# Local attention: row sums of the second bank of probabilities as one VectorE reduce in place of ScalarE's accumulator

## The reference

```python
for i in range(6):
    x = attn_layer(shift_tokens(x), Wqkv[i], q_scale[i], k_scale[i], Wo[i]) + x
    x = ffn_layer(shift_tokens(x), ...) + x

def attn_layer(x, Wqkv, qs, ksc, Wo):          # 16 heads of 64
    q, k, v = split(x @ Wqkv)
    q = rotary(l2norm(q) * qs); k = rotary(l2norm(k) * ksc)
    sim = einsum('bhwie,bhwje->bhwij', bq, bk2) * 8.0       # windows of 32, and the one before
    sim = where(mask, -max, sim)
    attn = softmax(sim, -1)
    return einsum('bhwij,bhwje->bhwie', attn, bv2) @ Wo
```

## Time and profile before

| | |
|---|---|
| median of 3 runs | 3133.28 us (3121.46 to 3135.31) |
| the profiled execution | 3126.73 us, span 3124.9 us |
| PE busy | 2713.3 us, 87% of the span |
| DVE busy | 2025.1 us, 65% |
| ACT busy | 1984.1 us, 63% |
| POOL busy | 1581.3 us, 51% |
| DMA queues | 5.5% of the 16 engines' span for the largest |

### The profile page before, as it was taken

The page is one execution under the profiler, slowest core; times in us unless marked ns, Lnnn a source line. Parts: engine busy times, 40 slices in busy tenths (PEclk is TensorE's granted clock), DMA queues, the critical chain, the costliest instruction groups (busy, mean ns, idle before and its releaser), DMA issues. The chain is left out here.

```text
span 3124.9 us, 70010 instructions
## 1 busy us (share of the span) xinstructions
PE 2713.3 (87%) x27218; PEld 1731.6 (55%) x27218; DVE 2025.1 (65%) x3872; ACT 1984.1 (63%) x5960; POOL 1581.3 (51%) x1845
## 2 busy tenths in 40 slices
PE   5996998899988998899889988999879977996995
PEld 2554776467746775577647764777434434552552
DVE  3765887588847885788668865888345434645663
ACT  3445888488857886688758884888523333554343
POOL 0424877288827883688548872888133102310530
PEclk8898999999999999999999999999979987998797
DMA  2001000100010001000100001000000000000000
GB/s 97 2 2 45 17 17 17 42 17 17 17 40 19 17 17 37 21 19 17 40 17 17 18 15 42 17 18 17 31 7 1 2 0 0 2 1 0 1 2 14
DMA packets 35939, 57.93 MB, mean 19 GB/s; under 512 B 7200, under 2 KB 32800, under 8 KB 33952
## 3 DMA queue, kind: packets, MB, share of 16 engines
q1 hardware_dynamic: 35616, 53.52, 5.5%
HBM read 27.28 MB, written 1.05 MB: 9 GB/s over the span
## 5 line engine op out<-in xcount | busy, mean ns | idle before, releaser
L1051 POOL TENSOR_TENSOR l_qk<-l_ta,l_tb 128x256 f32<-128x256 f32 x768 | 539.9, 735 | 110.3 <-DVE l_tb L1105 110.3
L1067 POOL TENSOR_TENSOR l_qk<-l_qk,l_rn 128x512 f32<-128x512 f32 x384 | 392.7, 1044 | 217.3 <-DVE l_rn L1127 217.3
L674 POOL TENSOR_SCALAR qmr<-q_all,cf 128x256 fp32r<-128x256 f32 x128 | 116.1, 926 | 710.8 <-SPq L475 375.7
L706 DVE TENSOR_REDUCE mrow<-ring 128x2 f32<-128x512 f32 x512 | 324.3, 683 | 196.6 <-PE ring L522 184.1
L972 ACT ACTIVATE l_pr<-st,l_mn 128x128 f32<-128x128 f32 x1152 | 407.5, 382 | 35.7 <-DVE l_mn L1093 35.7
L1058 POOL TENSOR_TENSOR l_pr<-l_pr,l_rs 128x512 f32<-128x512 f32 x384 | 391.7, 1042 | 43.0 <-DVE l_rs L1117 43.0
L659 ACT ACTIVATE pt<-st 128x512 f32<-128x512 f32 x384 | 200.2, 600 | 288.4 <-PE st L557 288.4
L1109 DVE TENSOR_REDUCE l_n<-l_sq 128x8 f32<-128x512 f32 x384 | 262.8, 686 | 178.0 <-ACT l_sq L981 175.9
L972 ACT ACTIVATION_READ_ACCUMULATOR l_pr<-st,l_mn 128x1 f32 x1152 | 255.3, 222 | 0.0
L547 PE MATMUL st<-qm,k_all 32*128 32x512 f32 x1024 | 223.0, 673 | 0.0
L835 PE MATMUL ring<-l_wa,l_xs 128*128 128x512 f32 x384 | 194.0, 628 | 24.2 <-DMA l_wa<-in_wa 13.1
(11 more groups left out here) (237 smaller groups left out, 6380.3 us busy)
## 6 DMA issues: line engine op xcount, KB each, us to landing
l_vm<-l_v SPq DMA_DIRECT2D x192, 96.0 KB, 2.0
l_wa<-in_wa SPq DMA_DIRECT2D x7, 2048.0 KB, 9.5
l_vm<-l_v SPq DMA_DIRECT2D x192, 32.0 KB, 1.9
l_wf<-in_wf SPq DMA_DIRECT2D x6, 580.5 KB, 3.7
w<-in_w SPq DMA_DIRECT2D x1, 2752.0 KB, 16.1
cf<-in_cf SPq DMA_DIRECT2D x1, 1123.0 KB, 17.8
x<-in_xT SPq DMA_DIRECT2D x1, 1024.0 KB, 4.8
ctxT<-in_ctxT SPq DMA_DIRECT2D x1, 1024.0 KB, 8.6
```

Source lines behind the costliest of these rows:

```text
L706: dve.tensor_reduce(mrow[b % 2][:, t, j, 2 * p:2 * p + 2], bank_of(f"R{r}").rearrange("p (h k) -> p h k", h=2), AX.X, ALU.max).then_inc(ri ...
L1051: ins = pool.tensor_tensor(halves[0][:, :, x], halves[1][:, :, x], halves[2][:, :, 1 - x], ALU.add)
L1067: pool.tensor_tensor(part, part, t.rn[:, :, 4 * x:4 * x + 4].unsqueeze(3).broadcast_to([P, 2, 4, LHD]), ALU.mult).then_inc(qk_normed, 1)
```

## The change

ACT's exponentials of the first bank (hh = 0) keep their accumulator output. Those of the second bank (hh = 1) have none. DVE's `reciprocals` first reduces the 4 x 128 exponentials of the second bank in SBUF to 4 sums in one instruction, raises a new semaphore, waits for it, and then takes the reciprocals of all 8 sums as before.

```diff
-    recip_ready, p_normed = g.sem("l_reciprocals_ready"), g.sem("l_probs_normed")
+    sums_ready, recip_ready, p_normed = g.sem("l_row_sums_ready"), g.sem("l_reciprocals_ready"), g.sem("l_probs_normed")
@@ exps (ACT)
                 for x in range(4):
                     c, tile = divmod(x, 2)
+                    kw = {"accum_out": t.ps[:, u, hh, x:x + 1]} if hh == 0 else {}
                     ins = act.activation(t.pr[:, u, hh, c, tile, :],
                                          bank(g, f"R{hh}", k)[:, x * P:(x + 1) * P], ACT.Exp, scale=-1.0,
-                                         bias=t.mn[:, u, hh, x:x + 1], accum_out=t.ps[:, u, hh, x:x + 1])
+                                         bias=t.mn[:, u, hh, x:x + 1], **kw)
                 ins.then_inc(exps_done, 1)
@@ reciprocals (DVE)
             def reciprocals(N, k):
                 dve.wait_ge(exps_done, 2 * N + 2)
+                dve.tensor_reduce(t.ps[:, k % 2, 1, :], t.pr[:, k % 2, 1, :, :, :].rearrange("p c t q -> p (c t) q"),
+                                  AX.X, ALU.add).then_inc(sums_ready, 1)
+                dve.wait_ge(sums_ready, N + 1)
                 dve.reciprocal(t.rs[:, k % 2, :, :], t.ps[:, k % 2, :, :]).then_inc(recip_ready, 1)
```

## The result

The kernel after takes 3056.09 us (median of 6 runs) against 3125.47 (6 runs of before): ratio 0.9772, 95% interval 0.9754 to 0.9791. The kernel after is 2.3% faster; 2.4% was forecast. One of its six executions took 3914.22 us, at a granted clock of 0.641 where the other five had 0.941 or 0.942; it moves the median by 0.3 us and is left out of the ratio. The profiled execution took 3054.89 us with a span of 3053.1 us; the span of before was 3124.9, so 71.8 us went.

A forecast was written before the change was run, and what follows sets the result against it. The prediction took plain steps (8.54 us) to be bound by a loop through the floor held by POOL. Savings of 16 x 0.67 + 6 x 0.15 + 6 x 0.14 = 12.5 us per pass, 75 in six, gave 3058 us, range 3037 to 3112.

The forecast's parts named there:

- Saving on ACT: Four exponentials per step without accumulator output: 0.09 us saved on each, 0.36 per step, bounds 0 and 0.68.
- Reduction: DVE's added 4 x 128 reduction from SBUF: 0.69 us like line 1109, 0.72 until the dependent instruction starts.
- Floor: DVE's floor on the norms: arrives at t+5.97 instead of t+6.33, t being the start of the step's minima.
- Boundary: Change from POOL's first probability multiplication to its second, at t+6.35; a floor arriving earlier slips in, freeing 1.0 us.
- Next bound: Line 1123 (1127 after) held to the end of POOL's pair, first loop 7.76 us; shift copy held, 1.20 us.
- Steps: Per pass, 16 plain steps 0.67 us shorter, 6 shift steps 0.15 and 6 with the addition into y 0.14.
- PE's own need: PE alone would need 7.81 us per plain step: 8.54 less its 0.73 wait for the copy of k.
- DVE's chain behind the reduction: Reduction at t+3.66, reciprocal at t+4.38, first sum of squares about t+4.61, second t+5.21, floor t+5.93.
- Shift steps: Steps with the shift's copy between floor and refinement: 8.36 us against 8.51, 0.15 less, 6 per pass.
- half the gain: Rival, chance 0.12: ACT saves only 0.15 to 0.2 us per step, or PE needs over 7.81; 43 us gained, 3090.
- No change: Rival, chance 0.13: the floor still misses POOL's boundary, plain steps stay at 8.54 us; 3128 to 3135 us.
- held reduction: Slower rival, chance 0.07: POOL holds DVE's added reduction, its pair starts 1.0 us later; 168 us more, 3300.

The follow-up runs named there:

- e1: The kernel before, with the floor on the norms as a reduction by maximum over pairs with a constant; 3092.57 us, ratio 0.989 to before.
- e9: The kernel after, with the floor as the reduction by maximum that e1 uses; 3044.6 us, ratio 0.974 to before.
- e12: The kernel after, with both banks reduced on DVE, floor and shift copies as reductions, addition into y between the rotary product pairs; 2999.69 us, ratio 0.961 to before.
- e3: The kernel after, with no exponential accumulating and DVE reducing both banks in one operation of 8 x 128; 3035.39 us, ratio 0.970 to before.
- e6b: The kernel after, with two copies 128 wide added on ACT between the exponentials and the squares; 3137.45 us, ratio 1.004 to before.
- e5: The kernel after without DVE's added reduction: second bank's exponentials don't accumulate and nobody sums them; 3044.97 us, ratio 0.975 to before.

## Why the prediction was right

Point by point:

- *Saving on ACT*: 0.36 us per step was forecast, 0.38 measured (4 x 0.095).
- *Reduction*: 0.69 was forecast, 0.674 measured; the reciprocal starts 0.70 behind it, not 0.72.
- *Floor*: it was to arrive at t+5.97, and does.
- *Boundary*: t+6.35 was forecast; POOL's pair starts at t+5.34, which makes it t+6.36.
- *Next bound*: line 1127 is held to the end of POOL's pair (median 376 ns), and the shift's copy takes 1.2 us, both as said.
- *Steps*: 7.87, 8.36 and 8.09 were forecast for plain, shift and y; 7.87, 8.37 and 8.07 were measured.
- *Sum*: 75 us was forecast, 71.8 measured in the spans.

By the figure of the Trainium skill ("ScalarE: Activation LUTs", *What ACT_TABLE_LOAD costs*) the exponentials would start 0.294 apart and the plain step would be 8.03. The trace has 0.25 and 7.87, so that figure gives too small a saving.

The rule that a floor slips in or is held was tested on far more than these rows. In the eleven traces whose floor is the old instruction (all but e1, e9 and e12) there are 1848 steps from k = 2 to 29. Take the boundary at 1.02 us behind the start of POOL's pair. The 1284 floors that arrived 0.11 us or more ahead of it ended 0.03 to 0.04 behind POOL's first multiplication. The 564 that arrived between 0.04 ahead and 0.08 behind ended as much behind the second. None arrived in between.

The closeness of the sum owes something to luck. The steady steps, k = 2 to 29, gave 75.4 us in the traces (1422.4 to 1347.0), as forecast. The first and last steps of the passes, set at nothing, gave another 6.5. But the stretches between the passes took 5.8 more, the one ahead of the first 1.8 and the one behind the last 2.5. These 10 us lost were not forecast. In the fourteen traces the stretch behind the last pass alone, where the kernels hardly differ, varies from 918 to 933 us.

Three terms were sized wrong, with little harm to the sum. **PE's own need** was taken as 7.81 from one step. It is 7.67: from one wait's end to the next, less the wait, the two rows of PE above give 1024.22 - 1016.35 - 0.20, and plain steps that follow each other in e1 and e12 give the same. (In the plain steps of before PE also loses 0.14 between lines 884 and 927, which shows in no bracket.) So the wait for the copy of k did not fall to 0.1 or less, as the prediction said: it is 0.20 in nine of the 16 plain steps of a pass and 0.36 in the other seven, those behind the addition into y among them. **DVE's chain behind the reduction** was set 0.1 late: the first sum of squares follows the reciprocal by 0.12, not 0.23. This hid behind the wait for ACT's square. It came out in e3, where that wait was gone and the error decided on which side of the boundary the floor fell. **Shift steps** are 7 in a pass, not 6, which is 1 us.

The rivals: *half the gain* needed a smaller saving on ACT or a PE above 7.81, and neither is there. *No change* is what e6b shows when ACT's saving is given back in front of the squares. The *held reduction* never happened (687 ns at most in 192).

## What to carry to other kernels

A tiny instruction with a long mean duration is a wait in disguise: look at what another engine does when it ends. Where one engine's operation can only slip in between two of another's, the edit that moves it over the boundary is worth up to a whole operation. So work out the arrival time and the boundary to better than a tenth of a microsecond, with all the links between, before pricing the edit; then ask which loop stands next. And don't take a gain for the busy time that was removed before you have given that work back at another place: 70 us of ACT's work fit the 72 here by chance.

## What the runs showed of the hardware

Of DVE's instructions with both ends in SBUF, those held by POOL here were the scalar operation (1.07 us for 16 elements), the copies (1.20) and line 1127 with its two SBUF inputs (0.38); reductions, over 32 to 1024 elements, never were (the 512-element ones took at most 0.69 us, the 1024-element ones 1.20 to 1.22), nor was the reciprocal of 8 (0.19 to 0.21). A reduction over an axis of one element is thus a copy that POOL did not hold, at 0.40 us for 256 elements where the copy takes 0.28 when free. Held instructions ended behind POOL's multiplication, the floor and line 1127 by 0.03 to 0.04 us, the copies by 0.15.

An accumulator output costs ACT 0.095 us of spacing on these 128-wide exponentials, though its read shows as an instruction of 204 ns.

What I had not expected: passes of the same code start differently. In the kernel after, the first step of a pass took 7.7 to 7.8 us in two passes and 9.0 to 9.2 in four, and the stretch between passes 69.0 to 71.6. Most of the 10 us by which after and e5 differ, with the same steady steps, lies there. Why a pass starts one way or the other stays open.
